# Router logits taken from the context products of a fused transformer step, a reordered attention stage and a new opening of it

## The reference, cut to what matters

```python
x = x + xattn(layernorm(x), ctx, ctx, mask, ...)       # 16 heads of 16
x = x + gated(layernorm(x), ...)                       # 4 of 16 heads of 64, chosen per batch entry
x = x + mlp(layernorm(x), ctx, ctx)
x = x + moe(layernorm(x), w_router, w1, b1, w2, b2)

def gated(x, ...):                                     # Q, K, V of the chosen heads
    score = softmax(einsum('bhqd,bhkd->bhqk', Qs, Ks) / sqrt(64))
    return einsum('bhqk,bhkd->bhqd', score, Vs) ... @ Wo + bo
def mlp(x, w1, w2):                                    # w1 = w2 = context
    g = gelu(einsum('eth,efh->etf', x, w1), approximate=True)
    return einsum('etf,efh->eth', g, w2)
def moe(x, w_router, w1, b1, w2, b2):                  # 8 experts, top 1
    logits = einsum('bsh,he->bse', x, w_router)
    sel, wgt = argmax(softmax(logits)), max(softmax(logits))
    return sum_e (sel == e) * wgt * (relu(x @ w1[e] + b1[e]) @ w2[e] + b2[e])
```

## Time and profile before

| | |
|---|---|
| median of 3 runs | 622.28 us (621.88 to 623.95) |
| the profiled execution | 622.69 us |
| its span, first to last instruction | 620.9 us |
| PE busy | 558.7 us (90%) |
| DVE / ACT / POOL busy | 450.6 / 356.1 / 263.6 us |
| mean granted clock of PE | 0.943 |
| gated attention | about 156 to 391 us of the span |
| context MLP and routing | about 391 to 464 us |
| experts | about 464 to 621 us |

### The profile page before, as it was taken

One profiled execution on the slowest core, in us unless ns is written; L12 is line 12 of the kernel. 1 busy time (PEld: TensorE's weight loads), 2 busy tenths in 40 slices (PEclk: granted clock), 3 DMA queues, 4 the chain that ended last, 5 costly groups with the idle time before them and its releaser, 6 DMA issues. The chain is left out here.

```text
span 620.9 us, 11787 instructions
## 1 busy us (share of the span) xinstructions
PE 558.7 (90%) x3619; PEld 495.4 (80%) x3620; DVE 450.6 (73%) x909; ACT 356.1 (57%) x727; POOL 263.6 (42%) x288
## 2 busy tenths in 40 slices
PE   4789999994899999999999998899648999999993
PEld 3679999983688888888888887766647899899992
DVE  4888888974138888889888987496664775785672
ACT  3468888753258887788777886035303642662351
POOL 4145545751024443444445343115426572683311
PEclk9879999997899999999999999897658999999998
DMA  8245422200522233222232200722415581671100
GB/s 255 60 119 153 128 52 51 52 1 1 129 51 52 52 73 81 53 51 52 57 84 65 53 1 0 278 99 69 137 30 221 217 287 35 215 250 44 38 26 0
DMA packets 25402, 57.00 MB, mean 92 GB/s; under 512 B 5112, under 2 KB 9977, under 8 KB 23304
## 3 DMA queue, kind: packets, MB, share of 16 engines
q1 hardware_dynamic: 21608, 48.80, 26.9%
q0 software_dynamic: 2256, 5.55, 3.0%
q10 hardware_dynamic: 1488, 2.05, 1.1%
HBM read 33.28 MB, written 4.87 MB: 61 GB/s over the span
## 5 line engine op out<-in xcount | busy, mean ns | idle before, releaser
L987 POOL TENSOR_SCALAR h_p<-h_p,h_rs 128x1024 f32<-128x1024 f32 x64 | 72.5, 1133 | 116.1 <-DVE h_rs L1082 116.0
L1089 DVE TENSOR_REDUCE h_nmx<-h_psS 128x1 f32<-128x1024 f32 x64 | 78.1, 1221 | 28.5 <-PE h_psS L1168 27.1
L1011 ACT CAST h_pTh<-h_psT 128x512 fp32r<-128x512 f32 x128 | 69.2, 590 | 31.3 <-PE h_psT L1126 31.1
L1069 DVE TENSOR_TENSOR h_pTl<-h_psT,h_pTh 128x512 fp32r<-128x512 f32 x128 | 81.4, 677 | 4.5 <-ACT h_pTh L1011 4.5
L1038 ACT ACTIVATE h_p<-h_psS,h_nmx 128x1024 f32<-128x1024 f32 x64 | 72.3, 1129 | 14.0 <-DVE h_nmx L1089 14.0
L1137 PE MATMUL h_psO<-h_pTh,h_vs 128*128 128x256 f32 x256 | 69.9, 306 | 3.0 <-DVE oT L1077 2.2
L1126 PE MATMUL h_psT<-ident,h_p 128*128 128x128 f32 x512 | 67.5, 273 | 1.4 <-DVE h_pTl L1069 1.2
L1126 PEld LDWEIGHTS h_psT<-ident,h_p 128*128 128x128 f32 x512 | 59.3, 141 | 11.4 <-issue 3.3
L1137 PE MATMUL h_psO<-h_pTl,h_vs 128*128 128x256 f32 x256 | 63.6, 282 | 0.0
L380 POOL TENSOR_TENSOR a_p<-a_p,a_rs 128x616 f32<-128x616 f32 x32 | 38.9, 1218 | 53.1 <-DVE a_rs L486 53.1
L1168 PE MATMUL h_psS<-h_kh,h_qs 128*128 128x512 f32 x128 | 55.7, 435 | 0.0
(11 more groups left out here) (318 smaller groups left out, 1406.6 us busy)
## 6 DMA issues: line engine op xcount, KB each, us to landing
wst<-in_m_w SPq DMA_DIRECT2D x16, 1024.0 KB, 5.0
bias<-in_m_b SPq DMA_DIRECT2D x8, 640.0 KB, 7.9
h_kh<-h_hi SPq DMA_DIRECT2D x30, 128.0 KB, 2.3
h_kl<-h_lo SPq DMA_DIRECT2D x30, 128.0 KB, 2.4
fw<-in_f_w SPq DMA_DIRECT2D x8, 384.0 KB, 4.0
rows<-x_all SPq DMA_DIRECT2D x4, 518.0 KB, 3.6
a_qs<-a_qhi SPq DMA_DIRECT2D x16, 128.0 KB, 2.3
a_qf<-a_qhi SPq DMA_DIRECT2D x16, 128.0 KB, 2.4
```

The lines of the kernel that those rows point to most:

```text
L987: pool.tensor_scalar(pr[:, u % 4], pr[:, u % 4], rs[:, u:u + 1], 0.0, ALU.mult, ALU.add).then_inc(pn_ready, 1)
L1011: act.copy(pTh[u // QP % 2][:, hf * HK:(hf + 1) * HK, u % QP * P:(u % QP + 1) * P], psT[hf][:]).then_inc(pT_hi, 1)
L1069: vec.tensor_tensor(pTl[u // QP % 2][part], psT[hf][:], pTh[u // QP % 2][part], ALU.subtract).then_inc(pT_lo, 1)
L1089: vec.tensor_reduce(nmx[:, u:u + 1], psS[u % 2][:], AX.X, ALU.max, negate=True).then_inc(max_ready, 1)
```

## The change

It has four parts.
1. **Opening of the gated stage.** `place` is cut into the moves of the high part and those of the low part; SP waits for each part alone. ACT issues only the three high moves of p=1, and DVE makes the first eight copies of V.
2. **The loop of the gated stage.** The four pieces of the next projection stood one behind the values of the second unit of four, two around the values of the third, one behind the scores of the fourth. Now two stand behind the scores of the third unit and two behind those of the fourth.
3. **Router logits by linearity.** The router is linear, so the logits of the updated x are those of the old x plus the update times the router columns. The old part rides in the hidden product: the context tile gets 8 more columns at 96 to 103 (wrc), zeros from 77 to 95, and psH 8 more rows, which ACT copies into `inner` behind the square. `mix` holds context times wrc (times 0.5) beside an identity; `route_update` multiplies `inner` by it, four matmuls of 16 columns a group, and gives both parts. DVE adds them, with the old part times the standard deviation. The second transposes, their ACT copies and `route` go. The four matmuls for mix stand behind the fifth attended product, and DVE copies mix ahead of its first normalisation. On DVE, six constants move ahead of the last gelu, the one-hot ahead of the last update, and the scaling before the exponential behind the `here` comparisons.
4. **Weights and bounds.** The lower halves of expert 1 go from POOL's MLP program to between its gathers of the experts' stage, the upper halves of its second matrix into ACT's MLP program. PE loads two bounds ahead of its first transposes, one behind them, and the other five before the first transposes of h.

The diff, cut to its core:

```diff
-        def place(eng, p):
+        def place(eng, p, part):
...
+            moves = ((qs, low_half, hi, low_half), (kh, low_half, hi, high_half), (kh, high_half, hi, high_half)), \
+                ((qs, high_half, lo, low_half), (kl, low_half, lo, high_half), (kl, high_half, lo, high_half))
+            for to, half, frm, from_half in moves[part]:
...
+                if p != 1:
+                    sp.wait_ge(qk_hi, p + 1)
+                    place(sp, p, 0)
                 sp.wait_ge(qk_lo, p + 1)
-                place(sp, p)
+                place(sp, p, 1)
...
-            for j in range(KT):
-                copy_v(j)
-                if j == 1:
-                    act.wait_ge(qk_lo, 2)
-                    place(act, 1)
+            act.wait_ge(qk_hi, 2)
+            place(act, 1, 0)
             split_v(0)
...
+            for j in range(KT):
+                vec.wait_ge(v_ps, j + 1)
+                vec.tensor_copy(v_all[:, 0:NA, j, :], vbank[j % 3]).then_inc(v_sb, 1)
...
-                if ahead and q % 4 == 3:
-                    project(ahead, 3)
+                if ahead:
+                    for piece in ((), (), (0, 1), (2, 3))[q % 4]:
+                        project(ahead, piece)
                 if u >= LAG:
                     transposes(u - LAG)
-                if ahead and q % 4 == 2:
-                    project(ahead, 1)
...
+        both, ctxs, wr = sb("c_both", [P, B, KD, RW]), sb("c_ctx", [L, B, D]), t["wr"]
+        ctxT = both[:, :, :, 0:L]
...
+            pool.memset(both[:, :, :, L:RA], 0.0)
...
             def square(n):
...
+                if n >= 2:
+                    act.wait_ge(r_ps, n - 1)
+                act.copy(inner[RA:RW, n % 2], psH[n % 2][RA:RW])
...
+            vec.memset(inner[HD2:RA], 0.0)
+            link(vec.memset(mix[:], 0.0))
+            vec.tensor_copy(mix[RA:, :, 1], ident[RA:RW, RA:RW].unsqueeze(1).to_broadcast([NE, B, NE]))
...
             attended(3)
+            vec.wait_ge(count_ps, 2)
+            vec.tensor_scalar(mix[0:L, :, 0], mix_in, 0.5, None, ALU.mult).then_inc(oh_ready, 1)
             normalise(0)
...
+            link(vec.tensor_tensor(logit[:], psR[:], std[:].unsqueeze(2).to_broadcast(full), ALU.mult))
+            link(vec.tensor_tensor(logit[:], psM[:], logit[:], ALU.add))
...
+            update(3)
+            spread(3)
...
+            vec.wait_ge(rstd_ready, 2 * NC)
+            vec.tensor_tensor(e[:], e[:], rstd4.unsqueeze(2).to_broadcast(full), ALU.mult).then_inc(shifted, 1)
             vec.wait_ge(exp_done, 1)
...
+            def route_update(n):
+                pe.wait_ge(g_ready, n + 1)
                 if n == 0:
-                    pe.wait_ge(y_sb, T // 2)
+                    pe.wait_ge(y_sb, T // 2 - 1)
                 for j in range(CH):
...
+                    ins = pe.matmul(products[:, n * CH + j], inner[:, n % 2, j * P:(j + 1) * P], mix[:, n // (NC // B)],
+                                    start=True, stop=True)
...
+                if 4 <= g < 6:
+                    low_first(pool, t, 1, g - 4)
...
-                    bounds(3)
+                    bounds(2)
                     transpose_x(0)
-                    bounds(2)
+                    bounds(1)
```

More of the change, by code:

```diff
@@ L42 @@
 UNIT = 1.5 * 2 ** 23
+RA = 96
+RW = RA + NE
 ENDS, TILES, LAST = 2 * TG, 2 * TG + NE - 1, 2 * TG + NE
@@ L1226, in context_mlp @@
         sq = sb("c_sq", [L, 2, CW])
-        later = sb("c_inner", [P, 2, CW])
-        inner = later[0:L]
-        spare = later[:].rearrange("p a q -> p (a q)")
-        e, first, rank = (spare[:, i * T * NE:(i + 1) * T * NE].rearrange("p (t e) -> p t e", e=NE) for i in range(3))
+        inner = sb("c_inner", [RW, 2, CW])
+        spare = flat[:, 2 * (2 * CH * D):]
+        e, first, rank, logit = (spare[:, i * T * NE:(i + 1) * T * NE].rearrange("p (t e) -> p t e", e=NE) for i in range(4))
         oh = sb("c_oh", [P, T + 1, NE], BF16)
@@ L1258, in context_mlp @@
         inverse = psC[:, 256:256 + TG]
-        shares_in = psR_bank[:, T * NE:T * NE + 2 * TG].rearrange("p (x g) -> p x g", x=2)
+        shares_in = psR_bank[:, 2 * T * NE:2 * T * NE + 2 * TG].rearrange("p (x g) -> p x g", x=2)
         column = psC[:, 384:384 + NE]
-        full_ones, wrc = sb("c_full_ones", [P, P]), sb("c_wrc", [P, KD, NE])
+        full_ones, wrc = sb("c_full_ones", [P, P]), both[:, :, :, RA:]
+        mix, std = sb("c_mix", [RW, B, 2, NE]), sb("c_std", [P, T])
+        mix_in = psO[0:L, 0, 0:B * NE].rearrange("p (b e) -> p b e", e=NE)
         names = ("dve", "pool", "consts", "var", "rstd_s", "xn_s", "xT_ps", "xT_sb", "h_ps", "sq_s",
@@ L1267, in context_mlp @@
              sem("c_" + n) for n in names)
-        order = [("mlp", 0), ("mlp", 1), ("mlp", 2), ("route", 0), ("mlp", 3), ("route", 1), ("route", 2), ("route", 3)]
         block = ctx.enter_context(nc.Block())
@@ L1360, in _ @@
             tanh(3)
-            copy_x("route", 1)
-            high_first(act, t, 1, 0)
-            copy_x("route", 2)
-            high_first(act, t, 1, 1)
-            copy_x("route", 3)
-            high_second(act, t, 0, 0)
-            high_second(act, t, 0, 1)
+            for hf in range(2):
+                high_first(act, t, 1, hf)
+            for e_ in range(2):
+                for x in range(2):
+                    high_second(act, t, e_, x)
             act.wait_ge(shifted, 1)
@@ L1448, in _ @@
             spread(1)
+            vec.scalar_tensor_tensor(std[:], mv[:, :, 1], EPS, rstd[:], ALU.add, ALU.mult)
             scaled(3)
-            update(2)
-            gelu(3)
-            spread(2)
-            update(3)
-            spread(3)
             vec.wait_ge(consts, 2)
@@ L1461, in _ @@
             link(vec.memset(steps[:, :, 0:1], -1.0))
-            vec.memset(steps[:, 0, 1:2], -1.0)
+            link(vec.memset(steps[:, 0, 1:2], -1.0))
+            gelu(3)
+            update(2)
+            spread(2)
             vec.wait_ge(r_ps, NC)
             full = [P, T, NE]
-            link(vec.tensor_reduce(best[:], psR[:], AX.X, ALU.max))
+            link(vec.tensor_tensor(logit[:], psR[:], std[:].unsqueeze(2).to_broadcast(full), ALU.mult))
+            link(vec.tensor_tensor(logit[:], psM[:], logit[:], ALU.add))
+            link(vec.tensor_reduce(best[:], logit[:], AX.X, ALU.max))
             most = best[:].unsqueeze(2).to_broadcast(full)
-            link(vec.tensor_tensor(first[:], psR[:], most, ALU.is_equal))
+            link(vec.tensor_tensor(first[:], logit[:], most, ALU.is_equal))
             link(vec.scalar_tensor_tensor(first[:], first[:], -float(NE), num[:, 0:NE].unsqueeze(1)
@@ L1561, in hidden @@
                 for k in range(KD):
-                    ins = pe.matmul(psH[n % 2][:], ctxT[:, n // (NC // B), k, :], xnT[:, i % 2, k],
+                    ins = pe.matmul(psH[n % 2][:], both[:, n // (NC // B), k, :], xnT[:, n % 2, k],
                                     start=(k == 0), stop=(k == KD - 1))
@@ L1594, in _ @@
                 attended(r)
-            transpose("mlp", 0)
+            pe.wait_ge(ctx_in, 48)
+            for b in range(B):
+                for k in range(KD):
+                    ins = pe.matmul(mix_in[:, b], ctxT[:, b, k, :], wrc[:, b, k], start=(k == 0), stop=(k == KD - 1))
+            ins.then_inc(count_ps, 1)
+            transpose(0)
             attended(5)
@@ L1886, in body @@
                 pe.reg_mov(second_at, e % 2 * FB * D)
+                if bounds:
+                    bounds(2)
                 pe.wait_ge(low2, 2 * (e + 1))
```

129 lines of the change are left out of this document (50 added, 79 removed).

## The result

The changed kernel takes 615.83 us, median of 4 runs (614.07 to 617.81); beside it the kernel before took 622.28. The ratio is 0.9892, 95% interval 0.9872 to 0.9913. The profiled execution took 615.31 us (span 613.6, mean clock 0.949), 7.4 less than the 622.69 of before. The forecast was 612.4, with 9.9 us gained.

A forecast was written before the change was run, and what follows sets the result against it. PE was taken to bound the gated loop and the experts, so only its waits could yield time. Opening 3.6, loop 0, MLP 5.6, bounds 0.7, experts 0 sum to 9.9 us gained: 612.4 us, range 609.0 to 618.1.

The forecast's parts named there:

- forecast case: Whole kernel: the likeliest outcome, 612.4 us with 9.9 gained, between 611.3 and 614; chance 0.5.
- rival (a): Clock falls twice in the MLP and the opening waits for transfers: 3.0 + 3.0 + 0.7 = 6.7 gained, 615.6; chance 0.15.
- Opening: 3.6: Gated stage's opening: transfers end near 167.6, 0.8 us earlier, first scores at about 167.8 to 168.0, 3.6 us gained.
- 3.0 for transfers that end no earlier: Gated stage's opening: gain if transfers still end at 168.5, from PE's lost wait and clock alone, 3.0 us.
- Loop: 0: Gated loop: reordered projection quarters change nothing, 0; bounds 6.3 us lost and 2 at most gained.
- (c): Gated loop: later transposes delay ACT, exp and DVE by two quarters a group, 12.6 us lost, 625.0; chance 0.04.
- (d): Gated loop: mild form of (c), 0.45 us a group, 6.3 lost, 618.7; chance 0.07.
- MLP: 5.6: Context MLP and routing: gather list earlier, 6.4 us gained less 0.8 for the clock, 5.6; bounds 3.0 and 6.4.
- the mix wait: MLP: DVE waits for four mix matmuls (0.98 us) ahead of its first normalisation; first transposes 2.4 us later.
- the 0.8 charged for a clock fall: MLP: half the 1.7 us price of PE losing full clock between 402 and 433, charged as 0.8.
- Bounds: 0.7: Experts' first transposes: one bounds load fewer ahead of them, 0.7 us gained; floor 0 if normalisation or moved loads show.
- Experts: 0: Experts: later gathers and fetches from moving POOL's lower halves of expert 1 cost 0; bound 2 us.

The follow-up runs named there:

- after: The changed kernel with all four parts, in its profile, against the kernel before: median 615.83 us, ratio 0.9892; profiled execution 615.31 us.
- open_alone: The kernel before with only part 1, the opening of the gated stage, changed: 620.11 us, ratio 0.9953 to the kernel before.
- act_six: The changed kernel with all six moves of p=1 issued by ACT: 616.11 us, ratio 0.9896 to the kernel before.
- loop_old: The changed kernel with the projection's quarters back in their old places in the loop: 615.99 us, ratio 0.9897 to the kernel before.
- mix_late: The changed kernel with DVE's copy of mix behind statistics(1) instead of ahead of normalise(0): 613.24 us, ratio 0.9840 to the kernel before.
- low1_back: The changed kernel with the lower halves of expert 1's first matrix back in POOL's MLP program: 616.82 us, ratio 0.9889 to the kernel before.
- bounds3: The changed kernel with three bounds ahead of the experts' first transposes and two behind, as before: 613.95 us, one run, no ratio.
- low_split: mix_late with one lower half of expert 1's first matrix behind the MLP's three gathers, the other behind the fifth gather: 611.50 us, ratio 0.9836 to before.
- small_low: The changed kernel with POOL's lower halves of expert 3's first matrix cut to 8 columns a part: 614.05 us, ratio 0.9850 to the kernel before.
- low_behind: mix_late with both lower halves of expert 1's first matrix behind the three gathers of POOL's MLP program: 612.82 us, ratio 0.9837 to before.
- low_ahead: mix_late with POOL's lower halves of an expert ahead of its gather in the experts' loop: 613.39 us, ratio 0.9839 to the kernel before.
- high2_back: The changed kernel with the upper halves of expert 1's second matrix back in ACT's experts program: 617.00 us, ratio 0.9888 to the kernel before.
- after_again: The changed kernel itself, unaltered, measured again in a later comparison: 615.93 us, ratio 0.9885 to the kernel before.

## Why the prediction was right, and where it was not

The time lies in the range and the direction was right. The forecast was 3.4 too low by medians, 2.5 by the profiled pair (9.9 against 7.4), of which 1.0 is the later start of the gated stage. By number the result lies outside the forecast case (611.3 to 614) and on rival (a), 615.6, but only the opening went as (a) says: the MLP gained 7.3 and not 3.0, and what took it back is a loss in the experts that no rival has. In the total, errors of +1.7 and -2.5 partly cancel.

**Opening: 3.6, measured 2.9.** The step that was mis-sized is from "168.4 - 0.8 = 167.6" to the first scores "at about 167.8 to 168.0". The transfers did end earlier: the DMA share falls to nothing 0.6 us earlier from the stage's start in after and 0.9 in open_alone, where 0.8 was forecast. But the scores follow that point by 0.9 to 1.0 us in each of the thirteen profiles in which PE waits for it, not by 0.2 to 0.4. The twelve profiles with this opening give 11.4 to 12.3 us to the first scores (median 12.1). The lower figure in the prediction, 3.0 for transfers that end no earlier, comes near by luck, for its reason is not what happened. The prediction took it from the Trainium skill, "DMA: Bandwidth & Descriptors", section "Issuing engines are not separate DMA queues", by which spreading the issues saves time on the issuing engines only. act_six agrees with that rule, with the same 7.9 us whoever issues; what came earlier is the start: SP's first move is issued at 160.96, 3.4 us behind the stage's first product, where it had been 3.95.

**Loop: 0, measured 0.12**, and 0.0 by loop_old. Rivals (c) and (d) are out. ACT's 1.48 us of idle is 1.04 in after, less by the one quarter, as the prediction said; DVE's 0.56 is 0.70, so it was not needed.

**MLP: 5.6, measured 7.3.** Four sizes: the mix wait cost 1.95 (13.30 - 11.35), not 2.4, since eight small matmuls take 0.66, not 0.98; the 0.8 charged for a clock fall behind 402 was not needed in this run; first transposes to sizes took 35.32 where the steps give 440.7 - 405.1 = 35.6; sizes to gather list 8.58 against 8.7. Together 1.7. That DVE's wait carries the loss was said in the prediction, and mix_late shows it: 1.69 of the 1.95 go with it. A fall at the place that rival (a) names did come in one profile, low1_back, but in place of the one near the start of the stage, not on top of it, so no profile shows the charge. No run separates the router's part of the 7.3 from the reorderings around it. What low1_back shows is that 2.9 of it hang on part 4 of the change: with expert 1's lower halves back in the stage the gain is 4.4 (66.46 - 62.07). The prediction had no term for that in the MLP; it came out near because its steps on DVE were taken without such a hold.

**Bounds: 0.7, measured 0.67 as a stretch and 0.1 to 0.2 net.** That is near the floor of 0 that the prediction named, but not for its reason: the loads in the body do not show, the half clock in it lasts longer (bounds3).

**Experts: 0, measured -2.5, beyond the bound of 2.** Here the prediction failed. The step was that POOL's lower halves of expert 1 may move because later fetches are "wanted a whole expert later". They are: no engine waits for weights. But the prediction asked only who waits for the data, not what runs beside what. The fetches issued at 465.18 and 471.55 fill the DMA engines (share 1.03 in 470 to 474, in low_split 0.61), POOL's first scatter waits until 478.31, POOL's next halves come 2.1 us later against the tiles, and fall on DVE's. Shown by experiment: the collision makes the gap (small_low), and the place of expert 1's halves makes the collision (low1_back, low_behind, low_split). Not shown: what holds POOL's scatter; the profile says only "issue". The full DMA engines alone do not: in low_ahead the share is 0.98 to 1.00 from 468 to 474, and the scatter starts at 472.62 after 1.90 us of idle. Of the 2.5, 1.8 is the gap (8.54 less 6.71) and about 0.6 stands in the first body (5.19 us from the first hidden product to the transposes of h, before 4.63), in which PE went back to full clock 4.6 us behind the first hidden product instead of 3.4.

The Trainium skill, "SBUF — State Buffer", section "Who interferes with whom", says that a DVE instruction with two inputs in SBUF contends with a GpSimd instruction that reads SBUF, and that the lock on the shared ports is exclusive. The rows agree: DVE's two instructions, 2.36 long elsewhere, end 2.23 us behind POOL's end at 489.17, and the one-hot 0.15 behind POOL's at 439.58. The instruction of 1.16 us at 434.46 has one input only, and it ended 0.02 behind POOL's all the same. With this in hand the prediction should have listed all pairs of such instructions and asked which the moved fetches bring together.

The spread of the changed kernel, 614.0 to 617.9, has one likely part in this: the gap is sometimes followed by half clock (mix_late and high2_back, with waits of 1.52 and 1.90 us and a second long distance of 8.17 and 8.11), sometimes not (after, after_again, loop_old, act_six and bounds3, with waits of 1.31 to 1.51). No profile of the changed kernel itself shows it, and seven profiles are too few for a rule. small_low and the kernel of open_alone, without the gap, spread over 1.5 and 2.4; low_split, without it too, over 3.6, so it is not the whole. Another part lies ahead of everything the change touches: the start of the gated stage, which differs by 3.3 us between the profiles.

## What to carry to other kernels

An operation moved off one chain has a second price where it lands: list which instructions of the other engines it may now run beside, and which DMAs it releases and when, and look at what these collide with, even if their data is wanted much later. Where a copy must wait for a product, place it at its use, not at its source: a wait and 0.17 us of work ahead of a normalisation cost 1.7. And a gain at the head of a stage is counted only at the end of the stage: the 0.67 us of the bounds were there in front and nearly gone one body later.

## What the hardware showed that I had not expected

- A DVE instruction of 0.29 us took 2.24 beside one POOL subtraction of 2.34 (low1_back): it ended with POOL's, whatever its own length. Others beside the POOL subtractions from 430.91 to 435.60 kept their time, such as the statistics (1.40 for four, 1.41 in after).
- The granted clock fell once near the start of the MLP stage in every profile, but not at the same place: between 388 and 397 in thirteen, behind the wait at 403.10 in low1_back. The price was the same, 1.7 us.
- The end of the DMA engines' activity is not yet the release of the engine that waits: PE went on 0.9 to 1.0 us later in all thirteen profiles in which it waits for the last transfer of the opening.
- POOL's first indirect scatter stood 5.3 to 6.2 us in the eight profiles with both halves between the gathers and the gather ahead of the next halves, 1.9 in low_ahead, and 0.3 to 0.4 where one or both halves were done earlier (low_split, low_behind, low1_back).
